# First attention: root iterations and routed norms to GpSimd and into the tail; first experts: first layer in fp16 parts

## What is computed

```
x = x + xattn0(layernorm(x), ctx, ctx, mask)     # 16 heads of 64, softmax over 512 keys, masked
x = x + ffn0(layernorm(x))
def ffn0(x):
    y0 = layernorm(x)
    scores = (tanh(xf @ gate_w.T) + 1) * 0.5
    vals, idx = top_k(scores.T, 256)             # each of 8 experts takes 256 rows
    y = layernorm(xf[idx]) * gamma + beta
    h = gelu(y @ fc1[e] + b1[e])                 # 256 -> 1024
    o = (h @ fc2[e] + b2[e]) * vals              # 1024 -> 256
    out = xf.at[idx].add(o)
```

## Time and profile before

| | us |
|---|---|
| median of 3 runs (lowest to highest) | 1168.98 (1166.55 to 1169.14) |
| the profiled execution | 1166.72 |
| its span in the profile | 1165.0 |
| mean granted clock of TensorE, share of full speed | 0.963 |
| first attention, by the timeline | 0 to about 531 |
| routing | about 531 to 569 |
| first experts, with the next projections | about 569 to 726 |

### The profile page before, as it was taken

One profiled execution on the slowest core, in us unless ns is written; L12 is line 12 of the kernel. 1 busy time (PEld: TensorE's weight loads), 2 busy tenths in 40 slices (PEclk: granted clock), 3 DMA queues, 4 the chain that ended last, 5 costly groups with the idle time before them and its releaser, 6 DMA issues. The chain is left out here.

```text
span 1165.0 us, 28797 instructions
## 1 busy us (share of the span) xinstructions
PE 1055.8 (91%) x10263; PEld 770.9 (66%) x10264; DVE 771.1 (66%) x2213; ACT 679.0 (58%) x1286; POOL 530.4 (46%) x599
## 2 busy tenths in 40 slices
PE   6999999999999999984799998598998866999996
PEld 3666777766776677673388885344454445888885
DVE  5888887898789987968501115667777774555553
ACT  5888876777768876757332226367667653343331
POOL 4677544464455433301336640566667523233312
PEclk9999999999999999995799999899999977999998
DMA  7633433333234433307736536514444241111110
GB/s 257 163 80 85 91 74 74 92 83 72 49 83 92 83 73 74 74 11 237 247 127 182 181 64 212 169 57 120 138 128 141 63 136 37 29 28 30 27 15 10
DMA packets 120028, 116.17 MB, mean 100 GB/s; under 512 B 43488, under 2 KB 100064, under 8 KB 119776
## 3 DMA queue, kind: packets, MB, share of 16 engines
q1 hardware_dynamic: 112608, 105.27, 32.0%
q0 software_dynamic: 7296, 9.25, 4.6%
HBM read 59.89 MB, written 21.82 MB: 70 GB/s over the span
## 5 line engine op out<-in xcount | busy, mean ns | idle before, releaser
L637 ACT ACTIVATE e<-masked,neg_max 128x512 f32<-128x512 f32 x256 | 184.4, 720 | 56.7 <-DVE neg_max L763 52.9
L737 DVE TENSOR_TENSOR e_t_lo<-et,e_t_hi 128x512 f16<-128x512 f32 x256 | 176.3, 689 | 39.9 <-ACT e_t_hi L630 38.1
L763 DVE CUSTOM_DVE_ANT_0 masked<-sc,mask_bias 128x512 f32<-128x512 f32 x256 | 175.2, 685 | 23.6 <-issue 21.6
L630 ACT ACTIVATE e_t_hi<-et 128x512 f16<-128x512 f32 x256 | 150.8, 589 | 59.0 <-PE et L510 58.0
L510 PEld LDWEIGHTS et<-ident,e 128*128 128x128 f32 x1024 | 123.2, 140 | 62.3 <-issue 15.1
L510 PE MATMUL et<-ident,e 128*128 128x128 f32 x1024 | 154.9, 274 | 2.3 <-ACT e L637 0.8
L2181 ACT ACTIVATE d_e<-d_st 128x384 f32<-128x384 f32 (+1 forms) x192 | 94.0, 526 | 48.5 <-PE d_st L2324 43.8
L73 PE MATMUL ob<-v_hi,e_t_hi 128*128 128x65 f16 x1024 | 119.0, 193 | 1.2 <-issue 1.2
L74 PE MATMUL ob<-v_lo,e_t_hi 128*128 128x65 f16 x1024 | 119.2, 193 | 0.0
L75 PE MATMUL ob<-v_hi,e_t_lo 128*128 128x65 f16 x1024 | 118.4, 193 | 0.0
L73 PE MATMUL h_hb<-h_xt_hi,experts_hi 128*128 128x256 f16 x352 | 96.6, 274 | 3.8 <-DVE h_xt_lo L2555 3.8
(11 more groups left out here) (486 smaller groups left out, 2761.3 us busy)
## 6 DMA issues: line engine op xcount, KB each, us to landing
kk<-nat_k SPq DMA_DIRECT2D x64, 256.0 KB, 3.5
raw<-in_fc SPq DMA_DIRECT2D x16, 1024.0 KB, 7.5
qq<-nat_q SPq DMA_DIRECT2D x64, 128.0 KB, 2.6
qk<-scratch_stack SPq DMA_DIRECT2D x64, 128.0 KB
scratch_stack<-kq_hi SPq DMA_DIRECT2D x16, 256.0 KB, 3.3
scratch_stack<-kq_lo SPq DMA_DIRECT2D x16, 256.0 KB, 3.5
d_expert_raw<-in_gate_w SPq DMA_DIRECT2D x8, 512.0 KB, 3.9
d_expert_raw<-in_up_w SPq DMA_DIRECT2D x8, 512.0 KB, 3.6
```

What stands on the lines that cost most here:

```text
L630: nc.scalar.activation(e_t[u % NBUF].hi[:], et[u % 2][:], ACT.Copy).then_inc(turned_hi, 1)
L637: nc.scalar.activation(e[u % NBUF][:], masked[u % NBUF][:], ACT.Exp, bias=neg_max[:, g % 2, j:j + 1], scale=-1.0).then_inc(exp_ok, 1)
L737: nc.vector.tensor_tensor(e_t[u % NBUF].lo[:], et[u % 2][:], e_t[u % NBUF].hi[:], ALU.subtract).then_inc(turned_lo, 1)
L763: nc.vector.tensor_tensor_reduce(masked[u % NBUF][:], sc[j % 2][:], mask_bias[g // PAIRS % 2][:, j % QT, :], -SCALE0, 3e38, ALU.add, ALU.m ...
```

## The change

In the first attention:

- DVE's late steps end with the bit guess; the three rounds and the shift are 14 small GpSimd steps (`newton_rounds`), each waiting for the one before, behind pair 3, unit 6 of a batch for "z" and pair 0, unit 3 for "r".
- "r" exists only for batches 0 and 1, with two steps in three units. GpSimd normalizes those rows in pair 1 and splits them in pair 2 of two batches later; SP turns the fp16 parts by four transposing transfers in pair 3 (`turn_routed`). The six "r" groups leave PE.
- Batch 2 gets its statistics, root, norm, transposes and split in the tail, like batch 3, ahead of the last pair's second normalization.

In the first experts:

- The first layer multiplies fp16 parts by `three_products`: 48 products for an expert in place of 16 fp32 ones. ACT makes the high parts of the turned rows (`turned_high`, one instruction of 128x512) and of the weights (`weights_high`, two of 128x1024), DVE the low parts.
- `load1(e)` waits for the low parts of expert e - 2 in place of its first layer.
- The weighed bias has three buffers in place of two, and GpSimd clears its stacks ahead of the scatter.

```diff
+    for kind, of in (("z", b + 1), ("r", b - 1)):
+        step = at - LATE_AT[kind]
+        n = step // 3 * 2 + step % 3
+        if of in LATE_OF[kind] and step >= 0 and step % 3 < 2 and n < LATE_STEPS[kind]:
+            return [(kind, of, n)]
     return []
...
+def newton_of(g, j):
+
+    p, b = g % PAIRS, g // PAIRS
+    if (p, j) == (3, 6) and b + 1 in LATE_OF["z"]:
+        return "z", b + 1
+    if (p, j) == (0, 3) and b - 2 in LATE_OF["r"]:
+        return "r", b - 2
+    return None
...
+                def turn_routed(b):
+                    cols = slice(b * S, (b + 1) * S)
+                    sp.wait_ge(pj_full, GROUP0["q", b * PAIRS + PAIRS - 1] + 1)
+                    sp.wait_ge(r_lo, 2 * (b + 1))
+                    for part, whole in zip(r_parts[b % 2], (T.z_t.hi, T.z_t.lo)):
+                        for c in range(DT):
+                            sp.dma_start(whole[:, c, cols].rearrange("p (t n) -> p t n", n=P), part[:, c, :], transpose=True).then_inc(r_turned, 16)
...
+                def newton_rounds(what):
+                    kind, b = what
...
+                    pool.wait_ge(late_ok, LATE0[kind, b, LATE_STEPS[kind] - 1] + 1)
...
+                    for n in range(3):
+                        step(pool.tensor_tensor(power, y, y, ALU.mult))
+                        step(pool.tensor_tensor(power, power, roots, ALU.mult))
+                        step(pool.tensor_scalar(power, power, -0.5, 1.5, ALU.mult, ALU.add))
+                        step(pool.tensor_tensor(y, y, power, ALU.mult))
+                    step(pool.tensor_tensor(power, y, mean, ALU.mult))
+                    step(pool.tensor_scalar(negative, power, -1.0, None, ALU.mult))
+
+                def norm_routed(b):
+                    pool.wait_ge(pj_full, GROUP0["w", (b, QT - 1)] + 1)
+                    for t in range(QT):
+                        pool.tensor_scalar(late_z[b % 2][t // 2][:, t % 2, :], T.x[:, b * QT + t, :], T.route_rstd[:, b, 0, t:t + 1], T.route_shift[:, b, 0, t:t + 1],
+                                           ALU.mult, ALU.add).then_inc(r_norm, 1)
...
+                    if u == units + 3:
+                        pe.wait_ge(turned_lo, units)
+                        turn_last(0)
...
+                    if u == units:
+                        dve.wait_ge(late_ok, len(LATE0))
+                        dve.wait_ge(newton, len(NEWTON0) * NEWTON_STEPS)
+                        for t in range(QT):
+                            last_statistics(B - 2, t)
+                        last_variance(0)
...
+                norm_last(0)
+                last_low(0)
...
                     stack_rows(sp, dram, T.kq[n], 1, n, T.keys_stacked)
                 for e in range(2, E):
-                    sp.wait_ge(h_full, GR * (e - 1))
+                    sp.wait_ge(fc1_lo, DT * (e - 1))
                     W.load1(sp, dram, e)
...
+                def turned_high(e):
+                    act.wait_ge(affine, e + 1)
+                    if e >= 2:
+                        act.wait_ge(h_full, GR * (e - 1))
+                    nc.scalar.activation(yt_parts[e % 2].hi[:], yt[e % 2][:], ACT.Copy).then_inc(yt_hi, 1)
+
+                def weights_high(e):
+                    act.wait_ge(W.fc1_in[e % 2], 16 * (e // 2 + 1))
+                    if e >= 2:
+                        act.wait_ge(h_full, GR * (e - 1))
+                    for c in range(DT):
+                        nc.scalar.activation(fc1_parts[e % 2].hi[:, c, :], W.fc1[e % 2][:, c, :], ACT.Copy).then_inc(fc1_hi, 1)
+
+                weights_high(0)
+                weights_high(1)
...
                 for n in range(KEYS_ROUTE, KEYS_FIRST):
                     act.wait_ge(keys_full, n - KEYS_ROUTE + 1)
                     nc.scalar.activation(T.kq[n].hi[:], kb[n % 2][:], ACT.Identity, bias=T.bqk[:, 1, n % DT:n % DT + 1]).then_inc(T.keys_hi, 1)
                 act.wait_ge(W.small_in, 64)
+                turned_high(0)
                 for e in range(E):
                     if e >= 2:
                         act.wait_ge(fc2_done, HALVES * (e - 1))
...
+                    if e + 1 < E:
+                        turned_high(e + 1)
+                    if e + 2 < E:
+                        weights_high(e + 2)
...
+                def turned_low(e):
+                    dve.wait_ge(yt_hi, e + 1)
+                    nc.vector.tensor_tensor(yt_parts[e % 2].lo[:], yt[e % 2][:], yt_parts[e % 2].hi[:], ALU.subtract).then_inc(yt_lo, 1)
+
+                def weights_low(e):
+                    for c in range(DT):
+                        dve.wait_ge(fc1_hi, DT * e + c + 1)
+                        nc.vector.tensor_tensor(fc1_parts[e % 2].lo[:, c, :], W.fc1[e % 2][:, c, :], fc1_parts[e % 2].hi[:, c, :], ALU.subtract).then_inc(fc1_lo, 1)
+
...
                     dve.wait_ge(T.keys_hi, n + 1)
                     nc.vector.scalar_tensor_tensor(out=T.kq[n].lo[:], in0=kb[n % 2][:], scalar=T.bqk[:, 1, n % DT:n % DT + 1], in1=T.kq[n].hi[:],
                                                    op0=ALU.add, op1=ALU.subtract).then_inc(T.keys_lo, 1)
...
                 for e in range(E):
                     if e + 1 < E:
                         scale_turned(e + 1)
+                        turned_low(e + 1)
+                    if e + 2 < E:
+                        weights_low(e + 2)
...
                 def first_layer(e):
-                    pe.wait_ge(W.fc1_in[e % 2], 16 * (e // 2 + 1))
-                    pe.wait_ge(affine, e + 1)
+                    pe.wait_ge(yt_lo, e + 1)
+                    pe.wait_ge(fc1_lo, DT * (e + 1))
...
                         for i in range(2):
                             f = 2 * g + i
                             for c in range(DT):
-                                mm = pe.matmul(hb[n % 2][:, i, :], W.fc1[e % 2][:, c, f * P:(f + 1) * P], yt[e % 2][:, c, :], start=(c == 0), stop=(c == DT - 1))
+                                cols = slice(f * P, (f + 1) * P)
+                                mm = three_products(pe, hb[n % 2][:, i, :], (fc1_parts[e % 2].hi[:, c, cols], fc1_parts[e % 2].lo[:, c, cols]),
+                                                    (yt_parts[e % 2].hi[:, c, :], yt_parts[e % 2].lo[:, c, :]), c == 0, c == DT - 1)
                         mm.then_inc(h_full, 1)
```

More of the change, by code:

```diff
@@ L137 @@
 LATE0 = {step: n for n, step in enumerate(step for u in range(PAIRS0 * UNITS) for step in late_steps(u))}
+NEWTON0 = {what: n for n, what in enumerate(what for u in range(PAIRS0 * UNITS) for what in [newton_of(u // UNITS, u % UNITS)] if what is not None)}
 EXPERTS0 = 8
@@ L448, in turn_norm, with turn_last @@
                     mm.then_inc(pj_full, 1)
[L450 to L457, removed]
+                def turn_last(n):
+                    for i in range(2):
+                        if i == 0:
+                            pe.wait_ge(z_dve, 2 * (n + 2))
+                        else:
+                            pe.wait_ge(r_act, 2 * (n + 1))
+                        for t in range(2):
+                            for c in range(DT):
+                                mm = pe.transpose(route_banks[n][i][:, c * 2 + t, :], last_z[n][2 * i + t][:, c * P:(c + 1) * P], T.ident[:])
+                        mm.then_inc(z_turned, 1)
                 def route(t):
@@ L597, in _ @@
                     late_products(qt, [CT - 1]).then_inc(late_full, 1)
-                pe.wait_ge(turned_lo, units)
                 pe.wait_ge(gate_lo, 1)
+                pe.wait_ge(r_turned, ROUTE_TURNED * (B - 2))
+                pe.wait_ge(z_lo, 4)
                 for t in range(NT - QT):
                     route(t)
+                turn_last(1)
                 for i in range(2):
[L603 to L612, removed]
+                    pe.wait_ge(z_lo, 4 + i + 1)
                     for t in range(2):
@@ L697, in _ @@
                     ahead = side_work((u + 2) // UNITS, (u + 2) % UNITS) if u + 2 < units else None
[L698 to L703, removed]
                     if ahead is not None and ahead[0] == "z":
                         b, i = ahead[1]
-                        act.wait_ge(late_ok, LATE0["z", b, LATE_STEPS - 1] + 1)
+                        act.wait_ge(newton, (NEWTON0["z", b] + 1) * NEWTON_STEPS)
+                        if b >= 3:
+                            act.wait_ge(r_lo, 2 * (b - 2))
                         if b >= 3:
@@ L1538, in _ @@
                         weigh_bias(e + 1)
-                    if e >= 1:
-                        scatter(e - 1, range(HALVES))
                     if 1 <= e <= QBUF:
@@ L1544, in _ @@
                         fill_constants()
+                    if e >= 1:
+                        scatter(e - 1, range(HALVES))
                 scatter(E - 1, range(HALVES))
@@ L1589, in _ @@
                 scale_turned(0)
+                turned_low(0)
                 for e in range(E):
```

196 lines of the change are left out of this document (115 added, 81 removed).

## The result

| | before | changed |
|---|---|---|
| median (lowest to highest) | 1169.06 (1166.55 to 1170.59), 4 runs | 1207.23 (1204.92 to 1208.26), 4 runs |
| ratio, 95% interval | | 1.0329 (1.0308 to 1.035) |
| span of the profiled execution | 1165.0 | 1203.2 |
| mean granted clock | 0.963 | 0.939 |

The change makes the kernel 3.3% slower, +38.2 us. The prediction was 1198 (1184 to 1213).

The account below looks back on a forecast made before the run. Both changed stages looked bound by PE (TensorE), with late VectorE steps delaying the attention and order deciding the experts. Attention -14.1 and experts +43.9 gave +29.8 on 1166.7, 1196.5; with 2.3 for the runs' median 1198.8, forecast 1198 (1184 to 1213).

Parts of the forecast that it names:

- The stall in the experts: First experts: PE stands 8.5 us awaiting gelus behind late-loaded weights; period about 23.0 us, +8.8, five times, +44.
- The clock: First experts, behind each stall: PE restarts at 1.2 GHz, is back after 3.7 us, and loses 1.9 us of work.
- First layer in fp16 parts: First experts: 48 fp16 products at 0.11 us take 5.27 against 6.91 us, -1.64 an expert if nothing waits.
- The opening and the tail: First experts' opening: first layer at 581.3, +2.5; first attention's tail: batch 2's transposes and root wait, +1.3.
- The attention: First attention with tail: -14.1 us in sum, last score product near 491 in place of 505.2.
- bounds of -7 and -17: First attention's sum: -7 if half of the excess has another cause, -17 if all goes.
- I let 4 of the 16.6 us stay ... That takes 12.6: First attention: of 16.6 us excess between score products in pairs with late steps, 4 stay and 12.6 go.
- the six groups that left PE: First attention: six groups of transposes leave PE, each 1.70 less 1.23 us, -2.8.
- nothing at 1 us each: First attention: GpSimd's 14 small steps and about 20 larger pieces per batch cost nothing, having 15 to 30 us before use.
- The rival on the attention: First attention: GpSimd's Newton steps or routed splits delay queued splits for PE, eating the -14: 1212 us, chance 0.06.
- The exclusive lock: First attention: VectorE and GpSimd share a port pair; by this nearly all excess goes, sum near -17.
- The other edits: First experts: third bias buffer and clearing ahead of the scatter, on GpSimd, cost nothing; uncovered, the clearing's own microsecond.

Follow-up runs that it names:

- q3_load_ahead: Changed kernel with plain transfers; SP loads expert e + 1's first-layer weights ahead of expert e's second-layer weights: 1153.92 us, 0.9868 of the kernel before.
- q8_ahead_newton_earlier: Against the changed kernel with plain transfers and first-layer loads issued earlier on SP: GpSimd's "z" Newton steps moved to pair 2, unit 7; 1152.41 us.

## Why the prediction was right, and where it was off

**The stall in the experts: right, in cause, place and size.** The chain was the one predicted: load at T + 0.61 (predicted 0.62), landed at T + 8.2 (8.6), third group at T + 11.0 (11.55), next transposes at T + 23.3 for this expert and T + 22.8 on average (23.0), with five waits of PE in all. ScalarE idled 13.56 us (14). q3_load_ahead shows that the order of two loads on SP decides it. Two sizes were off and offset each other. PE's wait was 7.8 us and not 8.5, above all because the load landed in 7.6 us and not 8.0. The clock cost more: in this expert the two groups behind the wait took 5.10 us (629.81 to 634.91) instead of 2.63, the second layer 7.24 instead of 6.91, together 2.8 us and not 1.9. That is one of the two dearest of the five. In the order of time they lost 2.3, 2.8, 1.4, 2.4 and 2.8 us, 11.6 in all and 2.3 on average. I had taken PE as back at full speed 3.7 us after the restart; in four of the five nearly all or all of the two groups, 5 us, ran at 1.2 GHz, in the third only the first 2.8 us.

**First layer in fp16 parts: right.** The spacing is 0.11 us, and an expert without a stall takes 12.59 us, 1.67 less than 14.26 (predicted 1.64). The Trainium skill's page "TensorE: Matmul & The Clock Gate", section "Back-to-back issue gap", gives figures for 128 and 512 columns from which I had estimated some 98 ns; the measured 110 ns decide.

**The opening and the tail: right** within 0.6 us each, +2.4 and +0.7 against +2.5 and +1.3. Low parts of the weights took 1.22 us each, against an estimate of 1.2.

**The attention: right in sign, half in size.** The last score product starts at 497.9 and not near 491, and with the tail the gain is 6.6 us, just outside the bounds of -7 and -17. (Those bounds don't follow from the terms beside them: with all 16.6 us gone the sum is -2.8 - 16.6 + 1.3 = -18.1, with half of the 12.6 it is -7.8.) The step that failed is "I let 4 of the 16.6 us stay ... That takes 12.6". In the pairs of that sum 8.6 us stayed, and the excess of the other pairs grew by 3.3, of which 2.8 in pairs 5 to 7. The sum gained 4.7, and with the 2.8 of the six groups that left PE this is the 7.5 us by which the first and the last score product have come closer. Two things were missed. The first is the cost that I had put at nothing, "nothing at 1 us each": I judged GpSimd by its idle half and by the time until the result is used, not by what is queued behind the steps. The rival on the attention named this very queue, but spread over all batches and with 1 us for a step. A step took 0.28, and PE's wait behind the block shows in batch 0 alone, where GpSimd also makes low parts of 2.15 us of the weights. Moving the block, q8_ahead_newton_earlier has 2.7 us less in pairs 4 and 5. The second is smaller: pairs 14 to 31 keep 5.4 us (1.1, 2.0 and 2.3) where I had allowed 4 for all. That these come from the statistics that remain is not tested; over the five traces with this attention they are 5.3 to 7.2.

**A rule from which too much was drawn.** The exclusive lock of the Trainium skill's page "SBUF — State Buffer", section "Who interferes with whom", was to make the attention's gain near 17 us, by way of the small products that leave VectorE. It was 6.6 with the tail. This does not speak against the lock itself (the last section shows it at work), but against the step from slow small products to idle time of PE. Why they were slow before was not tested.

**The other edits** were put at nothing. No wait of PE in the experts' stage of the changed kernel is put down to the third bias buffer or the clearing of the stacks; they were not tested alone.

## What to carry to other kernels

An engine with much idle time is not free: its program order is a queue. When work is put onto it, ask for each new instruction what it waits for and which instruction that others wait for now stands behind it; here high parts that need a load stood ahead of gelus that needed none, and the load stood behind a wait of its own on SP. The two orders together cost some 40 us, with ScalarE busy 57% of the span; another order on SP alone took it back. On a small scale 2.7 us went by the order on GpSimd, busy 47%. A new consumer that comes earlier than the old one also needs an earlier load: look at what the load itself stands behind before rewriting the consumer. And count an idle stretch of TensorE twice, once for its length and once for the products that run at half speed behind it.

## What the runs showed of the hardware

Against expectation, the conflict between VectorE and GpSimd showed above all on GpSimd's side. In q3_load_ahead VectorE's low parts of the weights, with two inputs in SBUF, stayed at 1212 to 1285 ns. A copy of two columns on GpSimd (0.18 us at 615.10 in the changed kernel) took 1.27 when it started together with such a low part. GpSimd's row and, below it, VectorE's:

```profile
618.96 1.27 POOL L1582 COPY slot_weight<-yg 128x2 f32<-128x2 f32 x1
```

```profile
618.96 2.36 DVE L1698 TENSOR_TENSOR fc_lo<-raw,fc_hi 128x1024 f16<-128x1024 f32 x2 [1.41 <-ACT fc_hi L1647]
```

This agrees with the Trainium skill's "SBUF — State Buffer", section "Who interferes with whom": the one that comes second stands until the other is done, here for about the 1.22 us of one low part. The next such copy fits too: it started at 632.42, 0.68 us into a low part, took 0.59 and ended 0.05 us behind it. It also happens the other way round. In q8_ahead_newton_earlier a low part that started at 628.95, 0.11 us behind GpSimd's product of the bias (128x256, 0.93 us), took 1.44 us in place of 1.22, as the prediction had thought possible.

In q3_load_ahead no instruction of PE waited for this. There is not much room, though: in q8_ahead_newton_earlier the transposes at 644.05 waited 0.44 us for the gathered rows, and that period was 13.19 us and not 12.59.

Behind 7.7 to 8.0 us of idle time TensorE ran at 1.2 GHz for the next 2.8 us in the shortest case and over 5.1 us in the longest, with the same instructions. With the stalls gone the granted clock of the stage was 1.00 again.
